# Summing the expert outputs of two token tiles in one GpSimd pass, with the other engines' steady orders changed

## The reference

```
attn = einsum('bqe,bke->bqk', xn Wq, xn Wk) * tril(ones)      # masked scores are 0, not -inf
att  = softmax(attn / sqrt(512)) @ (xn Wv)
gates = softmax(xn @ Wg)                                      # 8 experts
top 2 gates, divided by their sum, the others 0
ffn  = sum over e of gate_e * (xn @ We[e] + be[e])
out  = x + att + ffn
```

## Time and profile before

| what | value |
|---|---|
| median of 3 executions | 124.8 us (124.73 to 125.95) |
| the profiled execution | 125.6 us |
| its span on the core | 123.9 us |
| busy share PE, DVE, ACT, POOL | 93%, 86%, 81%, 73% |
| granted TensorE clock | 1.0 throughout |

### The profile page before, as it was taken

How to read it: one execution, slowest core, us unless ns; L and a number is a source line. 1 busy time by engine, 2 the same in 40 slices (tenths; PEclk the granted TensorE clock), 3 DMA queues, 4 the chain that set the end, 5 groups by cost and what they waited for, 6 DMA issues and landing times.

```text
span 123.9 us, 2936 instructions
## 1 busy us (share of the span) xinstructions
PE 115.3 (93%) x734; PEld 104.4 (84%) x734; DVE 106.8 (86%) x534; ACT 99.9 (81%) x338; POOL 90.4 (73%) x183
## 2 busy tenths in 40 slices
PE   4897949999999999999999999999999999999980
PEld 4787837998899998998999999999899888898960
DVE  0679869999989999898989898989989996969992
ACT  2456398989997999789987999799978998779910
POOL 7408848589957998489848995799848985863990
PEclk9999999999999999999999999999999999999999
DMA  3779300000300002000300020000200020000302
GB/s 102 238 213 281 98 3 5 0 3 3 85 0 0 8 12 72 0 0 3 90 3 0 0 85 5 0 0 15 77 0 5 0 85 0 0 3 0 93 0 85
DMA packets 9233, 5.18 MB, mean 42 GB/s; under 512 B 384, under 2 KB 9088, under 8 KB 9216
## 3 DMA queue, kind: packets, MB, share of 16 engines
q1 hardware_dynamic: 8656, 4.66, 13.1%
q10 hardware_dynamic: 560, 0.33, 1.0%
HBM read 2.89 MB, written 2.10 MB: 40 GB/s over the span
## 4 chain that ended last, share of the span: by engine, by line
PE 79%; POOL 5%; DVE 5%; DMA 3%; ACT 3%; issue 2%; ACTq 0%; DVEq 0%; POOLq 0%
PE attb L304 14%; PE ring L246 12%; PE ring L250 12%; PE ring L247 12%; PE score L291 6%; PE score L250 3%; PE score L247 3%; PE score L246 3%; DMA wqk_s<-in_w_attention_dram 3%; PE ring L313 2%; PE ring L323 2%; PE attb L347 2%; DVE mix L548 2%; POOL rhs_rows L1108 1%; PE score L354 1%
## 5 line engine op out<-in xcount | busy, mean ns | idle before, releaser
L886 ACT ACTIVATE ysc<-ring,gate 128x128 f32<-128x128 f32 x124 | 35.6, 390 | 1.9 <-PE ring L250 1.9
L246 PE MATMUL ring<-w_hi,xT_hi 128*128 128x512 f32 (+2 forms) x96 | 34.9, 364 | 0.1
L1066 POOL TENSOR_TENSOR ysc<-ysc 128x256 f32<-128x256 f32 x31 | 22.8, 736 | 15.4 <-ACT ysc L886 15.4
L247 PE MATMUL ring<-w_lo,xT_hi 128*128 128x512 f32 (+2 forms) x96 | 32.6, 340 | 0.0
L250 PE MATMUL ring<-w_hi,xT_lo 128*128 128x512 f32 (+2 forms) x96 | 32.6, 340 | 0.0
L1069 POOL TENSOR_TENSOR ysc<-ysc,mix 128x256 f32<-128x256 f32 x31 | 22.8, 735 | 3.7 <-DVE mix L548 1.4
L304 PE MATMUL attb<-c_s,probT 128*128 128x128 f32 x160 | 23.4, 278 | 0.0
L304 PEld LDWEIGHTS attb<-c_s,probT 128*128 128x128 f32 x160 | 21.4, 192 | 1.0
L548 DVE SCALAR_TENSOR_TENSOR mix<-ring,gate,mix 128x128 f32<-128x128 f32 x64 | 21.7, 342 | 0.4
L246 PEld LDWEIGHTS ring<-w_hi,xT_hi 128*128 128x128 f32 x96 | 18.2, 190 | 2.6 <-DVE mix L548 0.5
L905 ACT ACTIVATE prob<-score,nmx 128x128 f32<-128x128 f32 (+3 forms) x32 | 17.9, 558 | 2.8 <-DVE nmx L604 2.1
(11 more groups left out here) (107 smaller groups left out, 241.5 us busy)
## 6 DMA issues: line engine op xcount, KB each, us to landing
x_all<-in_x_dram SPq DMA_DIRECT2D x7, 256.0 KB, 4.4
out_dram<-o_s SPq DMA_DIRECT2D x7, 256.0 KB, 2.3
w_f<-in_w_stacked_dram SPq DMA_DIRECT2D x1, 256.0 KB, 4.2
w_f<-in_w_stacked_dram SPq DMA_DIRECT2D x1, 192.0 KB, 3.9
w_f<-in_w_stacked_dram SPq DMA_DIRECT2D x1, 132.0 KB, 3.7
x_all<-in_x_dram ACTq DMA_DIRECT2D x1, 128.0 KB, 2.8
x_all<-in_x_dram SPq DMA_DIRECT2D x1, 128.0 KB, 2.5
wqk_s<-in_w_attention_dram ACTq DMA_DIRECT2D x1, 128.0 KB, 3.8
```

The costliest lines, as they stand in the source:

```text
L246: nc.tensor.matmul(dst, hi, w_h, start=True, stop=False)
L247: nc.tensor.matmul(dst, hi, w_l, start=False, stop=False)
L886: last = nc.scalar.mul(ysc[:, t, e, :], bank(f"A{t}", b)[:, e * P:(e + 1) * P], gate[:, b % 2, t, e:e + 1])
L1066: chain.step(nc.gpsimd.tensor_tensor(y[:, 0:2, :], y[:, 0:2, :], y[:, 2:4, :], ALU.add))
```

## The change

POOL sums tiles 0 and 1 of a batch in one pass of three instructions, and tiles 2 and 3 in another (`sum_pair`); each instruction has twice the columns. The pass for tiles 0 and 1 waits until ACT and DVE have done tile 1, the other one until tile 3. Only the last batch still goes tile by tile. The first pass of a batch stands behind `scale_last`, as before; what was the third tile's sum in front of `bias_rows` goes with the fourth tile's, behind `normal_rstd`. The bodies of the loops of PE, DVE and ACT get new orders; prologue and last part of these three keep theirs.

```
-GROUPS = "B2- C3 A3- B3- SV DT- A0 B0 X+ A1 B1 C0+ U+ C1+ C2+ A2".split()
+GROUPS = "B2- C3 A3- B3- DT- SV A0 B0 X+ A1 B1 C0+ U+ C1+ C2+ A2".split()
@@ POOL
+            def sum_pair(b, h):
+
+                t, r = 2 * h + 1, slice(2 * h, 2 * h + 2)
+                y = ysc[:, r, :, :]
+                pool.wait_ge(S["a_used"], b * NT + t + 1)
+                chain.step(nc.gpsimd.tensor_tensor(y[:, :, 0:2, :], y[:, :, 0:2, :], y[:, :, 2:4, :], ALU.add))
+                pool.wait_ge(S["y7_ready"], b + 1)
+                pool.wait_ge(S["mix_ready"], b * NT + t + 1)
+                chain.step(nc.gpsimd.tensor_tensor(y[:, :, 0:2, :], y[:, :, 0:2, :], mix[:, r, 2:4, :], ALU.add))
+                if b > 1:
+                    pool.wait_ge(S["fin_done"], (b - 2) * NT + t + 1)
+                nc.gpsimd.tensor_tensor(ffn[:, b % 2, r, :], y[:, :, 0, :], y[:, :, 1, :], ALU.add
+                                        ).then_inc(S["ffn_ready"], 2)
...
             for n in range(1, B - 1):
                 normal_rstd(n + 1)
-                sum_experts(n - 1, 3)
+                sum_pair(n - 1, 1)
                 scale_last(n)
-                sum_experts(n, 0)
-                sum_experts(n, 1)
-                sum_experts(n, 2)
+                sum_pair(n, 0)
                 bias_rows(n)
 
-            sum_experts(B - 2, 3)
+            sum_pair(B - 2, 1)
             sum_experts(B - 1, 0)
@@ PE, loop body
+                scores(n, 0)
                 wide(n - 1, "B", 2)
...
-                scores(n, 3)
                 wide(n + 1, "C", 2)
@@ ACT, loop body
                 probs_copy(n - 1, 2)
+                gate_exp(n)
                 probs_copy(n - 1, 3)
-                gate_exp(n)
@@ DVE, loop body
                 token_sums_pairs(n)
+                token_sums_later(n)
...
+                sv_rows(n, 1)
+                finish_tile(n - 1, 0)
+                gate_out(n)
                 sv_rows(n, 2)
```

More of the change, by code:

```diff
@@ L399, in _ @@
                 attend(n - 1, 1)
+                transpose_probs(n - 1, 2)
                 wide(n - 1, "B", 3)
-                transpose_probs(n - 1, 2)
-                scores(n, 0)
                 transpose_probs(n - 1, 3)
+                scores(n, 1)
                 attend(n - 1, 2)
-                scores(n, 1)
+                transpose_rows(n - 1)
                 value_sums(n)
-                transpose_rows(n - 1)
                 attend(n - 1, 3)
@@ L410, in _ @@
                 wide(n, "A", 0)
+                transpose_probs(n, 0)
                 wide(n, "B", 0)
@@ L413, in _ @@
                 transpose_x(n + 1)
-                transpose_probs(n, 0)
                 wide(n, "A", 1)
+                scores(n, 3)
                 wide(n, "B", 1)
-                attend(n, 0)
                 wide(n + 1, "C", 0)
@@ L421, in _ @@
                 wide(n + 1, "C", 1)
-                scores(n, 3)
+                attend(n, 0)
                 wide(n + 1, "C", 2)
@@ L737, in _ @@
                 mix_b(n - 1, 1, 1)
+                negate_max(n - 1, 2)
                 mix_b(n - 1, 1, 2)
-                negate_max(n - 1, 2)
                 token_sums_pairs(n)
+                token_sums_later(n)
                 normal_stats(n + 1, 0)
+                normal_stats(n + 1, 1)
                 u_lo(n)
-                normal_stats(n + 1, 1)
                 mask_scores(n - 1, 3)
-                token_sums_later(n)
                 mix_b(n - 1, 2, 0)
                 normal_stats(n + 1, 2)
+                normal_stats(n + 1, 3)
                 mix_b(n - 1, 2, 1)
-                normal_stats(n + 1, 3)
                 negate_max(n - 1, 3)
-                mix_b(n - 1, 2, 2)
                 gate_max(n)
@@ L755, in _ @@
                 softmax_tot(n - 1)
+                mix_b(n - 1, 2, 2)
                 gate_below(n)
+                normal_finish(n + 1)
+                softmax_rec(n - 1)
+                gate_sum(n)
+                mix_b(n - 1, 3, 0)
+                mix_b(n - 1, 3, 1)
                 mask_scores(n, 0)
[L758 to L761, removed]
                 negate_max(n, 0)
-                mix_b(n - 1, 3, 1)
-                gate_rec(n)
-                gate_out(n)
                 mask_scores(n, 1)
@@ L768, in _ @@
                 negate_max(n, 1)
-                finish_tile(n - 1, 0)
+                gate_rec(n)
                 sv_rows(n, 0)
                 sv_rows(n, 1)
+                finish_tile(n - 1, 0)
+                gate_out(n)
                 sv_rows(n, 2)
+                mix_b(n, 0, 0)
+                mix_b(n, 0, 1)
                 finish_tile(n - 1, 1)
-                mix_b(n, 0, 0)
+                mix_b(n, 0, 2)
                 finish_tile(n - 1, 2)
-                mix_b(n, 0, 1)
                 finish_tile(n - 1, 3)
-                mix_b(n, 0, 2)
                 x_lo(n + 1)
@@ L991, in _ @@
                 probs_copy(n - 1, 2)
+                gate_exp(n)
                 probs_copy(n - 1, 3)
-                gate_exp(n)
                 scale_experts(n - 1, 3)
                 rows_copy(n - 1)
+                sv_high(n)
                 softmax_exp(n, 0)
-                sv_high(n)
                 normalize(n + 1)
                 scale_experts(n, 0)
+                probs_copy(n, 0)
                 x_hi(n + 1)
-                probs_copy(n, 0)
                 softmax_exp(n, 1)
@@ L1006, in _ @@
                 u_hi(n + 1)
+                masked_exp(n)
                 c_copy(n + 1, 1)
@@ L1009, in _ @@
                 c_copy(n + 1, 2)
-                masked_exp(n)
                 scale_experts(n, 2)
@@ L1142, in _ @@
             scale_last(0)
-            sum_experts(0, 0)
-            sum_experts(0, 1)
-            sum_experts(0, 2)
+            sum_pair(0, 0)
             bias_rows(0)
```

## The result

The changed kernel takes 131.8 us (131.59 to 131.85, 4 runs) against 124.9 us before (124.73 to 125.95, 4 runs): a ratio of 1.054, 95% interval 1.049 to 1.058. It is slower by 5.4%. The profiled execution's span went from 123.9 to 130.1 us, by 6.2 us; the medians differ by 0.7 more, since the execution profiled before was itself 0.8 us over its median.

A forecast was written before the change was run, and what follows sets the result against it. PE's matmuls were taken to bound the loop. Last part 1.2, six periods of 0.45 + 0.3, and one lost tie 1.15 made 6.85 us, on 124.8 giving 131.6 us; range 125.4 to 135.5.

The forecast's parts named there:

- The sign: Whole kernel: slower, with a chance of 0.72 for slower by over 1%.
- the likeliest case: Whole kernel: delays in the last part and loop plus one lost tie give 131.6 us; chance 0.52.
- the gates: Loop: gate_out on DVE is held by POOL's second 512-column step, so PE waits; 0.45 us a period.
- the token sums: Loop: DVE's L671 is held by POOL's first 512-column step, making u_lo late for PE; 0.3 us a period.
- the tie: Loop: DVE's L678 and POOL's next step start together; DVE loses once in six periods, +1.15 us.
- PE's orders: Loop: PE's new order of matmul groups costs nothing, within 0.1 us a period either way.
- the last part: After the loop: the pair pass ends 1.38 us later than the single sum, less 0.16 slack: +1.2 us.
- POOL's prices: The three instructions of a pair pass on POOL take 1.28, 1.28 and 0.74 us, 3.46 us in all.
- the rival that a step's price is mostly fixed: POOL's pair steps take under 0.75 us each, so the kernel is not slower, 124.0 us; chance 0.12.

The follow-up runs named there:

- third row first: The changed kernel with the third sv_rows moved ahead of gate_out on DVE: 131.5 us, ratio 1.054 to the kernel before.
- gates early: The changed kernel with gate_rec and gate_out put back ahead of the score masks on DVE: 128.6 us, ratio 1.030 to the kernel before.
- half pairs: The kernel before, in all its orders, with only tiles 0 and 1 of each batch summed in one POOL pass: 126.4 us, ratio 1.009.
- tail singly: The changed kernel with tiles 2 and 3 of batch 6 summed one by one in the old order: 131.0 us, ratio 1.050 to the kernel before.
- each half: Two kernels: the new PE, DVE and ACT orders with the old single sums, 135.7 us; the old orders with the pair sums, 133.7 us.

## Why the prediction was right, point by point

The sign, the likeliest case and the size were right: 131.6 forecast, 131.8 measured. The mechanism was right where it named the gates held by a longer POOL step, and the later last part. That the sum came out so close is luck: 2.95 of its 6.85 us (the token sums and the tie) were for things that cost nothing, and about as much was missing elsewhere (the gates, PE's orders, the last part).

**POOL's prices: right.** 1.28, 1.28 and 0.74 us forecast, 1.29, 1.29 and 0.74 measured, and not the 1.1 us of the estimate by the Trainium skill ("GPSIMD Engine Reference", section 3.1); the rival that a step's price is mostly fixed is gone.

**The gates, +0.45 a period: right place, size too small.** Its times were right within 0.06 us: `gate_out` forecast at 1.51 us behind the bias matmul (measured 1.56), the second step over at 2.54 (2.49), the copy of the probabilities ready at 3.9 (3.86). Two parts of the price were wrong. I let a quarter of the 0.6 us return, and nothing did. And I missed that the third `sv_rows`, queued behind `gate_out` on DVE, holds the bank of PE's second A group: GROUPS in the diff says so, with A1 four places behind SV. It is the same lateness as that of `scores(n, 3)`, as "third row first" shows, but PE meets it earlier. Taking the gates out of POOL's way gives back 0.71 us a period.

**The token sums, +0.3: wrong, it is 0.** L671 was to lose 0.35 us and loses 0.02 in the steady loop (0.25 in the first period). It comes 4.53 us behind the gates and POOL's step starts 3.39 behind them, where I had 4.4 and 3.5: both steps of the estimate were off by a tenth of a microsecond, and together they carry L671 to the last 0.15 us of the step. `u_lo` is in time.

**The tie, +1.15: wrong, it is 0.** L678 starts 0.03 us behind L671 and POOL's next step 0.10 us behind the first, and DVE got ahead in all six passes. The one lost tie in six came from the earlier trace rows, where nothing bound the two engines' instructions together; here L671 and POOL's first step end 0.02 us apart in every period, and DVE is the quicker each time. Being late by so little is nevertheless costly: with the gates early, L671 came 0.11 us behind a 512-column step in the last part and PE waited 1.06 us, and with half pairs L678 started 0.03 us behind L1073 and took 0.73 us.

**"PE's orders cost nothing": wrong by some 0.2.** With the hold gone, 0.23 us a period stays (13.67 against 13.45). It shows as waits of PE for the transposes, or, with the sums ahead of them, in the C groups. I had allowed 0.1 us either way. What of it is the order of the groups and what is lateness that comes from elsewhere is not shown.

**The last part, +1.2: right place, somewhat too small.** It was the length of the pass, 1.38 us, less slack. The last stretch lost 1.47 (the tail singly gives back 1.46), and the stretch before it 0.75 more, which falls to the loop's term. The pass took 3.52 us where I had 3.46, and it began 0.67 us ahead of the seventh bias matmul where the single sum had begun 0.97 ahead; I had let it start at the same place.

Together: six loop terms forecast at 4.5 and measured 5.25 (4.50 and 0.75), the tie 1.15 too much, the last part 0.27 too little. 4.5 + 1.2 + 1.15 = 6.85 against 5.25 + 1.47 = 6.72. The spans show 6.25 only because the execution profiled before had the later start of the two.

## What to carry to other kernels

When POOL's instructions get longer, list the small DVE steps with two inputs in SBUF that can fall beside them, and charge each with the rest of the POOL instruction, not with its own size. Then look at what is queued behind the held step: it may free a bank. Fewer, longer instructions on an engine with slack are no gain by themselves: here its saved microsecond a period was worth nothing, and splitting its steps again, which gives it more work, was worth 1.3 us.

An order that is written to fit one partner's timing is not a change of its own: each half of this one is slower than both together.

## What the runs showed of the hardware that I had not expected

A POOL instruction over few columns with much arithmetic held nothing: L1052, a power over four columns, lasts 1.02 us, and L533 ran beside it in 0.18. It did so in the kernel before too (0.19). So the rule of the Trainium skill ("SBUF — State Buffer", section "Who interferes with whom") that the later one is blocked wholly holds for the wide POOL steps here and not for this one. That a hold goes with the data read and not with the time is a guess.

Two POOL instructions of 256 columns without a wait between them take 1.42 us against 1.29 for one of 512, and a waiting DVE step gets in between: L533 ended 0.05 us after the first of them.

tensor_scalar on eight float32 columns was held just like tensor_tensor (0.96 and 0.70 us).
